# Four-layer graph network, fp32, one core: fewer matmuls in the layer 0 scores and in layer 1, blocks from GpSimd in every second lot

## What is computed

```python
# layer 0: W is adj (256 x 256), split in two halves of columns; bias is adj too
s1 = einsum('bkf,ef->bke', h, adj[:, :128]); s2 = einsum('bkf,ef->bke', h, adj[:, 128:])
pre = s1[:, :, None, :] + s2[:, None, :, :] + b_lin          # b, i, j, e: 256 x 256 x 256 a batch
e = einsum('bije,e->bij', where(pre >= 0, pre, 0.2 * pre), a) + adj
x = x + sigmoid(softmax(e, axis=2) @ h)
# layer 1 (h of the new x)
x_h = elu(h @ Wi + bi)
e = sigmoid(a_tgt[:, :, None] + a_src[:, None, :] + be) * mask
recv = elu(concat([e @ x_h, x_h * sum(e, -1)]) @ Wn + bn)
x = x + concat([recv, x_h]) @ Wm + bm
# layer 2: x + normalised exp(8 tanh(h q k' h' / ...)) * adj times h v
# layer 3: five steps of a gated update with adj @ h
```

## Time and profile before

| what | value |
|---|---|
| median of 3 runs | 5996.21 us (5992.98 to 6012.51) |
| the profiled execution's own time | 5989.9 us |
| its span in the profile | 5988.1 us |
| granted TensorE clock, mean | 0.996 of 2.4 GHz |
| TensorE matmul busy | 98% |
| ScalarE / GpSimd / VectorE busy | 88% / 82% / 81% |
| share of TensorE in the chain that ended last | 94% (line 1015 alone: 58%) |

### The profile page before, as it was taken

One profiled execution on the slowest core, in us unless ns is written; L12 is line 12 of the kernel. 1 busy time (PEld: TensorE's weight loads), 2 busy tenths in 40 slices (PEclk: granted clock), 3 DMA queues, 4 the chain that ended last, 5 costly groups with the idle time before them and its releaser, 6 DMA issues.

```text
span 5988.1 us, 128923 instructions
## 1 busy us (share of the span) xinstructions
PE 5885.9 (98%) x41812; PEld 2318.3 (39%) x41812; DVE 4837.7 (81%) x9171; ACT 5269.2 (88%) x12793; POOL 4916.4 (82%) x10392
## 2 busy tenths in 40 slices
PE   8999999999999999999999999999999999999997
PEld 2333333333334333333333333333433333333334
DVE  8978887888887888878888788888888887888873
ACT  8988898899988899888999889998889988899983
POOL 9988888888888888888888888888888888888880
PEclk9999999999999999999999999999999999999998
DMA  0000000000000000000000000000000000000000
GB/s 13 5 3 7 7 7 6 3 6 7 7 6 3 7 6 7 7 2 7 6 7 7 6 3 6 7 7 6 3 7 6 7 6 3 7 6 7 7 5 6
DMA packets 44353, 36.62 MB, mean 6 GB/s; under 512 B 4721, under 2 KB 39410, under 8 KB 43506
## 3 DMA queue, kind: packets, MB, share of 16 engines
q1 hardware_dynamic: 43506, 26.50, 1.5%
HBM read 9.71 MB, written 8.39 MB: 3 GB/s over the span
## 4 chain that ended last, share of the span: by engine, by line
PE 94%; ACT 2%; DVE 1%; POOL 1%; issue 1%; DMA 0%; SPq 0%; POOLq 0%; ACTq 0%; DVEq 0%
PE S L1015 58%; PE R L957 15%; PE S L957 6%; PE W L957 5%; PE R L1157 3%; PE PA L957 2%; ACT ring L812 2%; PE R L1165 1%; POOL ring L507 1%; PE PB L957 1%; PE S L1006 1%; PE S L1008 1%; DVE ring L613 1%; PE PB L1042 1%; PE PA L1023 0%
## 5 line engine op out<-in xcount | busy, mean ns | idle before, releaser
L507 POOL TENSOR_SCALAR ring<-W,U 128x256 f32<-128x256 f32 x9664 | 4686.4, 503 | 713.8 <-PE S L1015 642.2
L812 ACT ACTIVATE ring<-W,U 128x256 f32<-128x256 f32 x10272 | 4244.1, 503 | 13.3 <-PE S L1015 13.2
L1015 PE MATMUL S<-ring,a_window 128*32 128x512 f32 x32768 | 3750.1, 596 | 12.8 <-POOL ring L507 7.3
L613 DVE TENSOR_TENSOR ring<-U,W 128x512 f32<-128x512 f32 (+1 forms) x3840 | 3209.2, 862 | 155.5 <-PE S L1015 117.4
L1015 PEld LDWEIGHTS S<-ring,a_window 128*32 128x32 f32 x32768 | 952.2, 110 | 2269.6 <-issue 2245.4
L608 DVE TENSOR_TENSOR ring<-U,W 128x256 f32<-128x256 f32 x2464 | 993.6, 408 | 0.0
L957 PE MATMUL R<-mT,W 128*128 128x512 f32 (+1 forms) x640 | 339.1, 611 | 2.7 <-ACT mT L916 2.7
L957 PE MATMUL R<-AT,h 128*128 128x256 f32 x1260 | 316.8, 395 | 2.7 <-ACT h L928 2.1
L748 DVE SCALAR_TENSOR_TENSOR rh<-tr,h3T 128x512 f32<-128x512 f32 (+1 forms) x165 | 114.1, 692 | 240.2 <-ACT tr L919 240.2
L957 PEld LDWEIGHTS R<-AT,h 128*128 128x128 f32 x1260 | 230.4, 193 | 129.7 <-issue 100.6
L478 POOL TENSOR_TENSOR minus_mean<-mv,minus_one 128x4 f32<-128x4 f32 (+1 forms) x160 | 31.6, 197 | 272.3 <-DVE mv L676 216.8
(11 more groups left out here) (186 smaller groups left out, 4238.6 us busy)
## 6 DMA issues: line engine op xcount, KB each, us to landing
X<-in_x SPq DMA_DIRECT2D x64, 128.0 KB, 2.4
X_held<-X SPq DMA_DIRECT2D x32, 256.0 KB, 2.3
out<-OUT SPq DMA_DIRECT2D x64, 128.0 KB, 1.9
raw<-in_L_gnn_w_w SPq DMA_DIRECT2D x3, 128.0 KB
A<-in_adj SPq DMA_DIRECT2D x1, 256.0 KB, 2.7
Wn<-in_L_gnn_Wn SPq DMA_DIRECT2D x1, 128.0 KB
Wm<-in_L_gnn_Wm SPq DMA_DIRECT2D x1, 128.0 KB
rawu<-in_L_gnn_u_w SPq DMA_DIRECT2D x2, 64.0 KB
```

Source lines behind the costliest of these rows:

```text
L507: last = gp.tensor_scalar(ring[:, place, g, half * N:(half + 1) * N], W[:, y, c], LARGEST, U[:, y, c, i:i + 1], ALU.min, ALU.max)
L613: piece = dve.tensor_tensor(ring[:, place, g:g + groups].rearrange("p g (h j) -> p g h j", h=NB), u.unsqueeze(3).to_broadcast([P, groups, ...
L812: last = act.activation(ring[:, place, g, half * N:(half + 1) * N], W[:, y, c], ACT.Relu, bias=U[:, y, c, i:i + 1], scale=-1.0)
L1015: last = pe.matmul(S[y][g * ROWS:(g + 1) * ROWS, :], a_window[:, c, ROWS - 1 - row:2 * ROWS - 1 - row], ring[:, place, g], start=False, st ...
```

## The change

- The scores' remainder is the same for all rows: ScalarE now writes Relu(W - U_i), which is max(U_i, W) - U_i, and what depends on i alone drops out of the softmax. So `by_max`, its memsets, `lin_i`, the one-column matmuls of line 1031 and `exp_bias` go; `lin_w` is one 128 x 128 matrix; at the start of a half stands one matmul of 512 columns.
- ScalarE's bias is then -U: VectorE makes `U_minus` (512 elements a partition) after ScalarE's copy of U, and ScalarE's first block of a half waits for it.
- adj is no longer added by a matmul but in the maximum pass: two `tensor_tensor_reduce` of 256 elements on VectorE write -(S + A) to `neg_score` and its minimum to `neg_max`; the exp reads `neg_score` with scale -1. TensorE's next use of the bank waits for `max_ready`.
- Layer 1: GpSimd adds the two halves of `edge` (`halves`, lot 37), and one matmul of 512 columns with `ones` takes the place of four of 256. GpSimd adds bm + 0.5 to X1 (`shift`, lot 22), the residual reads `X1_shifted`, and the four one-row matmuls of L1 out go.
- GpSimd makes blocks in even lots only; the planner counts 2.0 more for each such start, and in odd lots splits between VectorE and ScalarE. TensorE waits for `by_pool` in even lots only.

```diff
-L1 = dict(project=26, exp=28, elu=29, ...
+L1 = dict(shift=22, halves=37, project=26, exp=28, elu=29, ...
-VECTOR_BLOCK, VECTOR_START, SCALAR_BLOCK, POOL_BLOCK = 2.67, 0.69, 3.57, 4.5
+VECTOR_BLOCK, VECTOR_START, SCALAR_BLOCK, POOL_BLOCK, POOL_START = 2.67, 0.69, 3.57, 4.5, 2.0
+POOL_EVERY = 2
@@ stage_costs
+    put(pool, L1, 0, shift=13, halves=13)
+def has_pool(t):
+    return t % POOL_EVERY == 0
@@ share_blocks
-        d, g, a = min(((d, BLOCKS - d - a, a) for d in range(1, BLOCKS) for a in range(1, BLOCKS - d)), key=ends)
+        if has_pool(t):
+            q += POOL_START
+            every = [(d, BLOCKS - d - a, a) for d in range(1, BLOCKS) for a in range(1, BLOCKS - d)]
+        else:
+            every = [(d, 0, BLOCKS - d) for d in range(1, BLOCKS)]
+        d, g, a = min(every, key=ends)
@@ GpSimd
-            gp.memset(by_max[:], 1.0).then_inc(mask_ones, 1)
...
+                if t == L1["shift"]:
...
+                    need(gp, x2_ready, turn.at(1, -1))
+                    gp.wait_ge(x1_ready, turn.at(2, 0))
+                    gp.tensor_tensor(X1_shifted[:], X1[:], bm_half[:].unsqueeze(1).to_broadcast([P, 4, P]), ALU.add).then_inc(x1_shifted, 1)
+                if t == L1["halves"]:
+                    gp.wait_ge(edge_ready, pair)
+                    gp.tensor_tensor(edge_sum[:].rearrange("p (y n) -> p y n", y=2), edge[:, :, 0], edge[:, :, 1], ALU.add).then_inc(edge_halves, 1)
...
-                    if turn.has_main:
+                    if turn.has_main and has_pool(t):
                         blocks(turn, t)
+                    if turn.has_l12:
+                        layer1(t, turn)
@@ VectorE
-                    dve.wait_ge(uw_psum, value)
-                    dve.tensor_copy(lin_i[:, y], PA[:, N:N + NB])
+                    dve.wait_ge(u_ready, value)
+                    dve.tensor_scalar(U_minus[:, y], U[:, y], -1.0, None, ALU.mult).then_inc(u_minus_ready, 1)
...
-                    dve.tensor_reduce(neg_max[:], S[y][:].rearrange("p (r j) -> p r j", r=NB), AXIS.X, ALU.max,
-                                      negate=True).then_inc(max_ready, 1)
-                    one_piece()
-                    dve.wait_ge(max_ready, value)
+                    need(dve, prob_ready, value - 1)
+                    dve.memset(score_carrier[:], 0.0)
                     for r in range(NB):
-                        last = dve.scalar_tensor_tensor(exp_bias[:, r:r + 1], neg_max[:, r:r + 1], lin_i[:, y, r:r + 1],
-                                                        lin_i[:, y, r:r + 1], ALU.subtract, ALU.add)
-                    last.then_inc(exp_bias_ready, 1)
+                        last = dve.tensor_tensor_reduce(neg_score[:, r], S[y][:, r * N:(r + 1) * N], A[:, r], -1.0, LARGEST,
+                                                        ALU.add, ALU.min, accum_out=neg_max[:, r:r + 1])
+                    last.then_inc(max_ready, 1)
...
+                    dve.wait_ge(x1_shifted, pair)
+                    dve.tensor_tensor(X2[:], S[1][:].rearrange("p (r d) -> p r d", r=4), X1_shifted[:],
                                       ALU.add).then_inc(x2_ready, 1)
@@ ScalarE
-                    act.wait_ge(u_ready, turn.at(2, y + 1))
+                    act.wait_ge(u_minus_ready, turn.at(2, y + 1))
...
                     last = act.activation(ring[:, place, g, half * N:(half + 1) * N], W[:, y, c], ACT.Relu,
-                                          bias=U[:, y, c, i:i + 1], scale=-1.0)
+                                          bias=U_minus[:, y, c, i:i + 1])
...
-                        last = act.activation(prob[:, r], S[y][:, r * N:(r + 1) * N], ACT.Exp, bias=exp_bias[:, r:r + 1],
+                        last = act.activation(prob[:, r], neg_score[:, r], ACT.Exp, bias=neg_max[:, r:r + 1], scale=-1.0,
                                               accum_out=row_sum[:, r:r + 1])
@@ TensorE
-                    need(pe, prob_ready, turn.at(2, y - 1))
+                    need(pe, max_ready, turn.at(2, y - 1))
...
-                    for r in range(NB):
-                        pe.matmul(S[y][:, r * N:(r + 1) * N], lin_w[:, y, r], H0T[:, y], start=r == 0, stop=False,
-                                  skip_group_check=True)
-                    pe.matmul(S[y][:].rearrange("p (r j) -> p r j", r=NB), ident[:], A_bias[:], start=False, stop=False,
+                    pe.matmul(S[y][:].rearrange("p (r j) -> p r j", r=NB), lin_w[:],
+                              H0T[:, y].unsqueeze(1).to_broadcast([P, NB, N]), start=True, stop=False,
                               skip_group_check=True)
...
-                pe.wait_ge(by_pool[place], turn.at(ROUNDS, rnd + 1))
+                if has_pool(t):
+                    pe.wait_ge(by_pool[place], turn.at(ROUNDS, rnd + 1))
...
-                    for r in range(NB):
-                        mm(PA[:, N + r:N + r + 1], H0T[:, y, r * P:(r + 1) * P], w_lin[:, 0:1])
...
-                    for y in range(2):
-                        for r in range(NB):
-                            last = mm(S[1][:, y * N:(y + 1) * N], ones[:], edge[:, y, r], r == 0, r == NB - 1)
-                    last.then_inc(agg1_psum, 1)
+                    pe.wait_ge(edge_halves, pair)
+                    mm(S[1][:], ones[:], edge_sum[:]).then_inc(agg1_psum, 1)
...
-                        mm(S[1][:, n * P:(n + 1) * P], ones[0:1, :], bm_half[:], True, False)
-                        mm(S[1][:, n * P:(n + 1) * P], recvT[:, n * P:(n + 1) * P], Wm[:, 0], False, False)
+                        mm(S[1][:, n * P:(n + 1) * P], recvT[:, n * P:(n + 1) * P], Wm[:, 0], True, False)
```

More of the change, by code:

```diff
@@ L59 @@
 LN1 = dict(stats=17, norm=19, transpose=20, copy=23)
-L1 = dict(project=26, exp=28, elu=29, edge_terms=31, edge_copy=33, tanh=33, mask=36, aggregate=39, agg_copy=42, receive=44, recv_exp=45, recv_elu=47, out=49, residual=52)
+L1 = dict(shift=22, halves=37, project=26, exp=28, elu=29, edge_terms=31, edge_copy=33, tanh=33, mask=36, aggregate=39, agg_copy=42, receive=44, recv_exp=45, recv_elu=47, out=49, residual=52)
 LN2 = dict(stats=56, norm=59, transpose=68, copy=70)
@@ L172, in node @@
     return half * P + g * ROWS + row
-def scalar_runs(y, c, n):
-    mine = [n >= BLOCKS - SHARES[y * LOTS_B + row * EC + c][2] for row in range(ROWS)]
-    edges = [row for row in range(ROWS) if mine[row] and (row == 0 or not mine[row - 1])]
-    ends = [row + 1 for row in range(ROWS) if mine[row] and (row == ROWS - 1 or not mine[row + 1])]
-    return list(zip(edges, ends))
 def gnn_stack(nc, x, adj, L0_b, L0_a, L1_Wi, L1_bi, L1_We, L1_be, L1_Wn, L1_bn, L1_Wm, L1_bm, L2_q, L2_k, L2_v,
@@ L275, in gnn_stack @@
         U = sb("U", [P, 2, EC, N])
+        U_minus = sb("U_minus", [P, 2, EC, N])
         W = sb("W", [P, 2, EC, N])
-        lin_i = sb("lin_i", [P, 2, NB])
         ring = sb("ring", [P, RING, GROUPS, NB * N])
@@ L284, in gnn_stack @@
         shift0 = sb("shift0", [P, NB])
+        score_carrier = sb("score_carrier", [P, 1])
+        neg_score = sb("neg_score", [P, NB, N])
         prob = sb("prob", [P, NB, N])
@@ L287, in gnn_stack @@
         neg_max = sb("neg_max", [P, NB])
-        exp_bias = sb("exp_bias", [P, NB])
         row_sum = sb("row_sum", [P, NB])
@@ L354, in gnn_stack @@
         pre_shift, h0_ready, h0T_psum, h0T_ready = (sem(n) for n in "pre_shift h0_ready h0T_psum h0T_ready".split())
-        uw_psum, u_ready, w_ready = (sem(n) for n in "uw_psum u_ready w_ready".split())
-        max_ready, exp_bias_ready, prob_ready = (sem(n) for n in "max_ready exp_bias_ready prob_ready".split())
+        uw_psum, u_ready, w_ready, u_minus_ready = (sem(n) for n in "uw_psum u_ready w_ready u_minus_ready".split())
+        max_ready, prob_ready = sem("max_ready"), sem("prob_ready")
         probT_psum, probT_ready, inv_ready, half_inv_ready = (sem(n) for n in "probT_psum probT_ready inv_ready half_inv_ready".split())
@@ L371, in gnn_stack @@
         agg1_psum, aggT_ready, selfT_ready = (sem(n) for n in "agg1_psum aggT_ready selfT_ready".split())
+        x1_shifted, edge_halves = sem("x1_shifted"), sem("edge_halves")
         recv_psum, recv_exp, recv_min, recvT_ready = (sem(n) for n in "recv_psum recv_exp recv_min recvT_ready".split())
@@ L463, in _ @@
                              pattern=[[-1, P]], channel_multiplier=1).then_inc(gp_const, 1)
-            gp.memset(by_max[:], 1.0).then_inc(mask_ones, 1)
-            gp.wait_ge(mask_ones, 1)
-            for y in range(2):
-                for c in range(EC):
-                    for n in range(BLOCKS):
-                        g, half = group_half(n)
-                        for first, end in scalar_runs(y, c, n):
-                            last = gp.memset(by_max[:, c, y, half, g * ROWS + first:g * ROWS + end], 0.0)
-            last.then_inc(mask_set, 1)
             gp.wait_ge(dve_const, 1)
@@ L509, in blocks, with layer1 @@
                 last.then_inc(by_pool[place], 1)
+            def layer1(t, turn):
+                pair = turn.at(1, 0)
```

(16 more changed lines are left out.)

40 lines of the change are left out of this document (12 added, 28 removed).

## The result

| | before | after |
|---|---|---|
| median of 4 runs each | 5998.40 us (5992.98 to 6012.51) | 5923.65 us (5913.85 to 5928.69) |
| profiled execution: own time / span | 5989.9 / 5988.1 us | 5913.85 / 5912.0 us |
| granted TensorE clock, mean | 0.996 | 0.993 |

The ratio is 0.987, with a 95% interval of 0.9848 to 0.9891: **faster by 75 us, 1.3%, where 166 us had been forecast**, and outside the range of 5802 to 5884. The profiled executions differ by 76 us. So 102 us of the priced 178 are missing; the forecast had set 12 of them aside for a stall.

A forecast was written before the change was run, and what follows sets the result against it. TensorE was taken to bound the loop; its removed work, 178 us, less 12 us for a stall of TensorE on ScalarE's blocks, gave 166 us less, a median of 5830 us, with a range of 5802 to 5884.

The forecast's parts named there:

- Edge sums: Layer 1 sums on TensorE: eight instructions of 1.73 us become one matmul of 0.86, saving 0.87 us a turn.
- Output: Layer 1 output stage on TensorE: 24 instructions (4.22 us) become 16 (1.99), saving 2.23 us a turn; lower bound 1.41.
- the thin place: ScalarE across the turn's end: its 2.5 us lead at lots 7 to 9 vanishes; stall 0.4 us a turn, 12 us.
- Rival C: Output stage stays slow without the one-row matmuls, saving only 1.41 us a turn: 5856 us; chance inside the forecast's 0.72.
- What bounds the kernel now: TensorE bounds the loop, idle 1.3 us a turn at the loop's edge; whatever leaves its stream leaves the time.
- U_minus: VectorE's instruction behind ScalarE's U copies, for which ScalarE's lot 0 waits: bound 0 to 0.5 us, taken as 0.
- Every second lot: GpSimd makes up to 6 blocks in an even lot, 2.9 us against two lots of TensorE; price 0.
- Start of a half: TensorE's first matmuls of each half: 0.93 us saved in one, 0.86 in the other, 1.79 a turn.
- Rival A: ScalarE runs short in several places, turn's end and middle, 2.6 us a turn: 5901 us, 5858 at the wrap alone; chance 0.18.
- Rival B: ScalarE's waits are round trips that stay, so it becomes the bound: 6133 us, slower; chance 0.05.
- Rival D: Shares or an unseen maximum instruction make VectorE late at lot 5, eating the gain: 5990 us; chance 0.05.
- The two adds on GpSimd: Layer 1 adds of 512 elements, 0.97 to 1.94 us each, taken as covered: price 0; uncovered, up to 62 us.

The follow-up runs named there:

- e4: The kernel before with the layer 1 half of the change alone (GpSimd adds, one sums matmul, no one-row matmuls); 5894.73 us.
- e13: e11 with layer 0's attention aggregate, tanh and residual one lot later; 5806.79 us.
- e8: The kernel before with two turns in the loop's body; 5970.91 us.
- e5: The changed kernel with the matmul at the start of a turn done twice, the second overwriting the first; 5917.57 us.
- e6: The changed kernel with VectorE's negation of U two lots later and four turns in the loop's body; 5863.66 us.
- e3: The changed kernel with two turns in the loop's body; 5887.68 us.
- e10: e6 with the planner's block costs set to those measured, giving ScalarE fewer blocks; 5826.97 us.
- e11: e10 with GpSimd making blocks in every lot; 5810.70 us.
- e1: The changed kernel with VectorE's negation of U two lots later; 5893.66 us.
- e2: The changed kernel with GpSimd making blocks in every lot again, with no start cost in the planner; 5899.50 us.
- e9: The changed kernel with both the negation of U two lots later and GpSimd's blocks in every lot; 5876.89 us.

## Why the prediction was wrong

**The prices of the matmuls were right.** *Edge sums* 0.86 and *Output* 1.98 (priced at 1.99) stand in the chain, and e4 gives 98.9 us of 99.2. The start in the other half is 0.86, and the U matmuls take 1.06 (1.13 priced). Behind an edge, too, the start gives its price where the supply does not stop: 1.12 + 6.15 = 7.27 us in e13 for before's 8.14, 0.87 of 0.93. The half without the gap in it shows the sum of the layer 1 prices: the way from the first matmul of y = 0 to that of y = 1 fell from 98.9 to 95.8 us in e4, 3.1 as priced. And where the edges and the thin place are gone, a turn takes 177.6 us (e13) against 183.0 (e8), 5.4 of the 5.65 priced, though e13 also differs in the shares. Rival C was wrong.

**The step that failed is the reading of the loop's edge** in "What bounds the kernel now": "That is the loop's edge, 1.3 us a turn", taken as a fixed sum, and with it "whatever leaves its stream leaves the time". The earlier trace rows show what is left of a branch of 3.5 us after what TensorE has in its queue. That is no constant but a difference, and the change cut what stood on both sides of it:
- *Ahead of the branch*: **U_minus**, priced at 0 to 0.5 us with VectorE's next pieces named behind it. It was asked whether VectorE's own time suffices, not what the instruction waits for: 181.9 us in 64 waits, with lot 127 behind it. The gap grew from 1.24 to 2.70, 1.46 a turn. **Every second lot**, priced at 0, has its share in it: with it undone, 12 instructions are queued, with both undone 20.
- *Behind the branch*: **Start of a half**, 0.93 of its 1.79. In the changed kernel the supply of instructions stops a second time there, and in before it does not. From the turn's first matmul to the 56th instruction of lots, before takes 1.13 + 0.86 + 6.15 = 8.14 us and after 1.12 + 0.98 + 1.09 + 6.20 = 9.39: 1.25 more in place of 0.93 less, 2.2 at this edge. In e5 an instruction put back there costs nothing. Why this code has the stop and before's and e13's have not stays open (table under e5).
- *The clock*: in 13 of after's 28 steady turns TensorE runs at the lower level (1.2 of 2.4 GHz) for a stretch after the gap, in one of before's. The stretches after the gap at 3225.01, with the clock in the third column from the right:

```profile
3220.00:3225.00 5.00, 5.00 (x48) 1.30 (x40) 4.13 (x6) 5.00 (x14) 2.75 (x6) 1.00 0.04 8
...
3230.00:3235.00 5.00, 5.00 (x38) 2.07 (x39) 5.00 (x11) 5.00 (x16) 4.77 (x11) 0.81 0.01 3
3235.00:3240.00 5.00, 5.00 (x43) 1.86 (x39) 5.00 (x10) 4.00 (x11) 5.00 (x12) 1.00 0.00 0
```

The first half of those 13 turns takes 97.0 us, that of the 15 others 96.3, so the lower clock costs about 0.7 us each time, some 9 us in all. The fall of the mean from 0.996 to 0.993 would by itself be 18 us of 5912, but TensorE stands idle in part of that time. In after's three other executions the mean was 0.988 to 0.990, with spans of 5920.4 to 5926.7 us, so part of the spread between runs may be the clock's.

Together they account for the gap between forecast and result: a steady turn takes 182.1 us where 184.3 - 5.65 = 178.65 were due, 3.5 more, times 28 edges 97 us, of the 102 that are missing. The half with the edge in front of it alone shows 96.6 where 98.9 - 4.4 = 94.5 were due (2.1 behind the branch, clock included); the half that ends at the edge 85.6 where 85.4 - 1.24 = 84.2 were (the 1.4 ahead of it). So more was lost behind the branch, 59 us, than ahead of it, 39.

**The thin place** was right in its engine and stretch, though half of it is the wait for `probT` and not for blocks, and in the measured kernel it hardly counted (5.6 us for `probT`, 9.1 for blocks), since ScalarE could catch up during the edge. With the edges gone it costs more than the 0.4 us a turn that were taken: e6's pure turns are 2.7 us above e13's. **Rival A** thus comes true only in part and as a consequence of the cure: ScalarE runs short at the wrap alone, in the turn's first half (97.5 us in e6, 94.8 in e13). The second half takes 82.8 us in e3, e6, e10, e11 and e13 alike, so "several places" was wrong. **Rival B** was wrong: ScalarE's idle time fell from 719 to 520 us (400 had been forecast) while TensorE stayed at 97%. **Rival D** too, as far as it named the maximum: this instruction, a row of after that before did not have, takes 415 ns, at the lower end of 0.41 to 0.69 us (48.6 us for 128); its accumulator read of 0.08 us lies beside it.

**The two adds on GpSimd** take 1.29 us each, between the bounds of 0.97 and 1.94, and TensorE has no wait for `edge_halves`:

```profile
L510 POOL TENSOR_TENSOR X_shifted<-X,bm_half 128x512 f32<-128x512 f32 x32 | 41.3, 1292 | 0.0
L513 POOL TENSOR_TENSOR edge_sum<-edge 128x512 f32<-128x512 f32 x32 | 41.1, 1285 | 97.9 <-DVE edge L693 97.9
```

The estimate of 1.1 us from the Trainium skill's "GPSIMD Engine Reference" was 15% low here, and its advice against such adds did not bear on a queue with room.

## What to carry to other kernels

A small wait without a releaser, once per loop iteration, can be the rest of a longer one: look how many instructions the bounding engine has queued when it reaches the branch, and what it executes right behind it. Anything that makes the last inputs of an iteration late can come back as idle time at the branch, and work taken away behind it gives its price only where the supply of instructions keeps up: nothing in e5's place, all of it in e13. So keep new waits away from the last lots of an iteration, put several iterations into one body where the program's size allows it (e3: 31 us for no change in the work), and expect the next thinnest place to show when the edge no longer gives it time.

## What the runs showed of the hardware

- A taken branch takes 3.3 to 4.6 us on TensorE's sequencer and 0.04 to 0.07 us on the four others, in the same loop; TensorE's last one, which is not taken, 0.08 us in every run. The Trainium skill's "Advanced Engine Details and Errata", Control Flow Timing, gives about 108 ns for a compare and branch, and no value of the traces agrees. The Trainium skill's "Runtime: NRT & Kernel Launch", Instruction fetch mechanics, says that a taken branch to a page outside the current two must first fetch the target by DMA. TensorE's 3.5 us taken against 0.08 not taken would fit that; that it is the fetch was not measured, and it does not say why the others branch fast.
- Behind the branch the supply stops a second time, for 0.45 to 1.2 us, in all five kernels with one turn in the body and the new layer 0 start (after, e1, e2, e5, e9), where the clock stays high. It does not in before, e4, e8 and e13. What decides this stays open.
- TensorE fell to its lower clock behind 12 of 13 edges in e3 (gap 2.70 us), 13 of 28 in after (2.70), 10 of 28 in e5 (2.57) and in e2 (2.09), 6 of 28 in e1 (2.10), and behind none in e9 (1.66), e4 (1.41) and e13 (1.37). In before (1.24) it was one of 28, behind the longest gap there, 2.20 us.
- The longest queue of matmul instructions seen at a branch is 20, in every kernel whose last lot is ready in time. In e1, e9 and e11 the branch takes 4.0 us in the median, in all others 3.4 to 3.7, e6, e10 and e13 with the negation later among them. This stays open.
- GpSimd in every second lot costs 16 to 19 us against every lot (e2 against the change, e9 against e1, e11 against e10). Part is the queue at the edge; in e11 against e10, with full queues and 6 edges, 0.7 us a turn remain, with `probT` later. What makes it later was not tried.
